# Moving the scan convolutions of six image pairs from TensorE to GpSimd

## The reference

```python
x = x + softmax(q @ k.T / 8) @ v                 # L0: attention over channels
x = relu(bn(deformable_conv3x3(x)))              # L1: offsets and mask from a 3x3 convolution
x = x + proj(softmax(q.T @ k / 8) @ v)           # L2: attention over the 256 pixels
# L3
y = depthwise3x3(layernorm2d(x)) + dw_b
for each of 4 directions (left-right, right-left, top-bottom, bottom-top):
    o += (conv1d_depthwise_5taps(y) + b) * sigmoid(y @ gate_w + gate_b)   # the "scan"
x = x + fuse(o)
x = x + ff2(a * sigmoid(g)),  a, g = split(ff1(layernorm2d(x)))
```

## Time and profile before

| | |
|---|---|
| time, median of 3 runs | 303.65 us (303.19 to 303.67) |
| span of the profiled execution | 301.8 us; the median lies 1.85 us above it |
| PE busy | 287.8 us (95%) |
| DVE busy | 213.0 us (71%) |
| ACT busy | 190.4 us (63%) |
| POOL busy | 53.0 us (18%) |
| TensorE clock granted | full in all 40 slices |
| from issue to landing, a load and a store of 128 KB (median) | 2.1 and 1.7 us |
| chain that ended last | PE 85%, DVE 5%, ACT 5%, POOL 1% |

### The profile page before, as it was taken

The page is one execution under the profiler, slowest core; times in us unless marked ns, Lnnn a source line. Parts: engine busy times, 40 slices in busy tenths (PEclk is TensorE's granted clock), DMA queues, the critical chain, the costliest instruction groups (busy, mean ns, idle before and its releaser), DMA issues.

```text
span 301.8 us, 7399 instructions
## 1 busy us (share of the span) xinstructions
PE 287.8 (95%) x2870; PEld 183.7 (61%) x2870; DVE 213.0 (71%) x424; ACT 190.4 (63%) x399; POOL 53.0 (18%) x139
## 2 busy tenths in 40 slices
...
DMA packets 3057, 4.98 MB, mean 16 GB/s; under 512 B 336, under 2 KB 2768, under 8 KB 2896
## 3 DMA queue, kind: packets, MB, share of 16 engines
...
...
HBM read 3.47 MB, written 1.05 MB: 15 GB/s over the span
## 4 chain that ended last, share of the span: by engine, by line
PE 85%; DVE 5%; ACT 5%; issue 3%; POOL 1%; ACTq 0%; POOLq 0%; DVEq 0%
PE ps_cv L534 22%; PE ps_pair L615 11%; PE ps_yb L494 8%; PE ps_pair L480 7%; PE ps_ma L437 6%; PE ps_ma L464 4%; PE ps_mb L580 3%; PE ps_pair L602 3%; PE ps_pair L570 3%; PE ps_mb L591 3%; PE ps_mb L547 3%; PE ps_mb L388 2%; PE ps_pair L635 2%; PE ps_mb L624 2%; PE ps_yb L374 1%
## 5 line engine op out<-in xcount | busy, mean ns | idle before, releaser
L901 DVE TENSOR_TENSOR sb_wt<-ps_yb,sb_xe 128x512 f32<-128x512 f32 x144 | 94.0, 684 | 26.4 <-PE ps_xb L489 24.9
L534 PE MATMUL ps_cv<-sb_wt,sb_w_x 128*64 128x256 f32 x576 | 77.3, 385 | 0.0
L740 ACT ACTIVATE sb_xe<-ps_xb 128x512 f32<-128x512 f32 x72 | 43.0, 597 | 19.3 <-PE ps_xb L489 19.2
L534 PEld LDWEIGHTS ps_cv<-sb_wt,sb_w_x 128*64 128x64 f32 x576 | 38.2, 136 | 20.2 <-issue 7.5
L615 PE MATMUL ps_pair<-sb_y_pad,sb_par 64*128 64x256 f32 x320 | 37.4, 383 | 0.3 <-ACT sb_gates L799 0.3
L615 PEld LDWEIGHTS ps_pair<-sb_y_pad,sb_par 64*128 64x128 f32 x320 | 30.9, 184 | 5.8 <-issue 2.5
L942 DVE SCALAR_TENSOR_TENSOR sb_dw_acc<-sb_z_pad,sb_par,sb_dw_acc 128x256 f32<-128x256 f32 x56 | 25.2, 480 | 9.4 <-ACT sb_dw_acc L792 5.3
L494 PE MATMUL ps_yb<-sb_hats,sb_sel 32*128 32x512 f16 x144 | 29.8, 383 | 0.7
L1039 POOL TENSOR_TENSOR sb_parts<-sb_hat,sb_parts 128x256 f16<-128x256 f32 (+2 forms) x40 | 23.3, 615 | 38.7 <-ACT sb_parts L710 38.6
L1046 POOL TENSOR_SCALAR sb_sc<-sb_mv 128x1 f32<-128x1 f32 x16 | 3.0, 190 | 142.1 <-DVE sb_mv L936 74.7
L489 PE MATMUL ps_xb<-sb_hats,sb_sel 32*128 32x512 f16 x72 | 27.7, 385 | 0.2 <-ACT sb_hats L719 0.2
(11 more groups left out here) (117 smaller groups left out, 438.4 us busy)
## 6 DMA issues: line engine op xcount, KB each, us to landing
...
```

The source lines that it names most:

```text
L534: mm = nc.tensor.matmul(cv[C * b:C * (b + 1), 0:PIX], w_x[n % 2][:, b, h, k, :], wt_of(n, k, h)[:, PIX * b:PIX * (b + 1)], start=(k == 0 a ...
L740: nc.scalar.activation(xe[t % XE][:, :], xb[:, :], ACT.Copy).then_inc(ev("xe_ok"), 1)
L901: nc.vector.tensor_tensor(wt_of(n, k, h)[:, :], yb[h][:, :], xe[t % XE][:, :], ALU.mult)\
```

## The change

For pairs 1 to 6 (`BY_POOL`) the scan is no longer done by PE and ACT. DVE writes `y` to a dense tile; SP issues four DMAs of 64 KB that put both images' channels on both halves of the partitions (`y_dup`); POOL then does for each of the two axes five multiply-and-add instructions by a column of weights (the first with the bias, straight into `conv`, the others into `tap_of` with a column of zeros added) and four additions into `conv`. That is 18 POOL instructions for a pair, each on 512, 480 or 448 elements for a partition. `prod` then waits for POOL's last addition on each axis. Pairs 7 and 8 keep their scans on PE.

Besides: `z_pad`, `dw_acc`, `y_pad`, `gates`, `conv`, `prod`, `z2`, `ff_a`, `ff_g`, `ff_u` get two buffers, `x4` three, `x2` eight, with the waits for freed buffers set accordingly; two more memsets on DVE at the start; `HOT` sums to 29 in place of 46, `WARM` to 22 in place of 21; and all lists of steps are written anew. In the new lists:

- DVE has `y.1` after `w5a.3` (before: after `w8a.3`), `y.6` after `w2a.8`, and behind the last weights `w8b.8`: `dw2.7 dw4.7 out.5 dw6.7 dw3.7 dw5.7 dw7.7 prod.6 max.8 x4.6 dw8.7`, later `dw7.8 dw8.8 y.8 prod.7`.
- POOL has each `ln1` inside the scan of the pair before, for instance `mul12.2 ln1.3 mul03.2 sum12.2 mul13.2 sum03.2 sum13.2 mul04.2 mul14.2 sum14.2 sum04.2`, and `low.5` to `low.8`, `ln2` and `x1` between or inside the scans.
- PE has `... sp_last.8 hot.1 ff2.5 s8a.8 s8b.8 gate.6 qk2.8 hot.2 logit.8 ...`: no `scan.6`, and `gate.6` behind the last sampling step.
- SP has `load.3 load.4 load.5 load.6 dup.1 dup.2 store.1 dup.3 load.7 dup.4 store.2 load.8 store.3 dup.5 dup.6 store.4 ...`.

```diff
+BY_POOL = (1, 2, 3, 4, 5, 6)
+ORDER = (2, 1, 3, 0, 4)
+SUMS = 2 * KS - 1
+            def dup(n):
+                sp.wait_ge(ev("y_ok"), n)
...
+                for b in range(2):
+                    for i in range(2):
+                        sp.dma_start(y_dup[n % 2][C * i:C * (i + 1), b, :, :].rearrange("p h w -> p (h w)"),
+                                     y[n % 2][C * b:C * (b + 1), :])\
+                            .then_inc(dup_ok[n % 2], 16)
...
+            def scan_times(d, i):
+                def step(n):
+                    rows, sum_of, tap_to = scan_rows(n, d, ORDER[i])
+                    weight = col("scan_c", KS * d + ORDER[i])
+                    if i == 0:
+                        pool.wait_ge(dup_ok[n % 2], 64 * len([k for k in BY_POOL if k <= n and (n - k) % 2 == 0]))
+                        wait_past(pool, ev("prod_ok"), n - 2)
+                        nc.gpsimd.tensor_scalar(sum_of, rows, weight, col("scan_b", d), ALU.mult, ALU.add)\
+                            .then_inc(ev(f"scan_step{d}"), 1)
+                    else:
+                        pool.wait_ge(ev(f"scan_step{d}"), scan_step(n, d, 2 * i - 2))
+                        nc.gpsimd.tensor_scalar(tap_to, rows, weight, col("none"), ALU.mult, ALU.add).then_inc(ev(f"scan_step{d}"), 1)
+                return step
+
+            def scan_plus(d, i):
+                def step(n):
+                    rows, sum_of, tap_to = scan_rows(n, d, ORDER[i])
+                    pool.wait_ge(ev(f"scan_step{d}"), scan_step(n, d, 2 * i - 1))
+                    nc.gpsimd.tensor_tensor(sum_of, sum_of, tap_to, ALU.add).then_inc(ev(f"scan_step{d}"), 1)
+                return step
...
             def prod_step(n):
+                wait_past(dve, ev("fuse_mm"), n - 2)
                 dve.wait_ge(ev("gate_ok"), n)
-                dve.wait_ge(ev("scan_ok"), n)
+                if n in BY_POOL:
+                    for d in range(2):
+                        dve.wait_ge(ev(f"scan_step{d}"), scan_step(n, d, SUMS - 1))
+                else:
+                    dve.wait_ge(ev("scan_ok"), made_by(BY_PE, n))
```

More of the change, by code:

```diff
@@ L60 @@
[L60 to L64, removed]
@@ L75 @@
[L75 to L78, removed]
+        warm.1 qk.1 warm.2 attn.1 warm.3 at.1 warm.4 mix.1 warm.5 x1.1 warm.6 off.1 prep.1 off_t.1 qk.2 wx0.1 attn.2
@@ L83 @@
[L83 to L96, removed]
+        attn.1 at.1 mix.1 off.1 prep.1 abs.1 tanh.1 attn.2 wx0.1 high.1 at.2 wx2.1 tr0.1 mix.2 xe0.1 tr1.1 xe1.1 tr2.1
@@ L97 @@
     """,
     "dve": """
[L99 to L102, removed]
@@ L113 @@
[L113 to L117 removed]
+        qk.1 a_max.1 a_norm.1 x1.1 dist.1 qk.2 a_max.2 hat.1 hat_y.1 a_norm.2 qk.3 low.1 x1.2 w0a.1 a_max.3 w0b.1 w1a.1
```

282 lines of the change are left out of this document (180 added, 102 removed).

## The result

The kernel with the change takes 310.3 us (median of 4 runs, 308.3 to 311.3), the kernel before 303.7 (4 runs, 303.2 to 304.5): a ratio of 1.021, 95% interval 1.018 to 1.023. It is slower, and the predicted 309 lies 1.3 us off. The profiled execution has a span of 308.0 us, against 301.8.

The account below looks back on a forecast made before the run. PE sets the pace before; afterwards DVE, waiting for POOL, was to bound the window. 301.8 + 8.7 - 4.7 + 2 = 307.8 us of span, plus 1.85 to the median about 309.7, said as 309; range 285 to 321.

Parts of the forecast that it names:

- window +8.7: From the first `y` to the last weights product: (124.7 + 29)/0.93 = 165.3 us, 8.7 us longer than before.
- tail -4.7 + 2: After the last weights product: 4.7 us less without a PE scan, plus 2 us for `prod.6` and `max.8` waiting.
- turns: POOL and DVE instructions reading two SBUF tensors, or scaling SBUF to SBUF, exclude each other, whole instruction by whole instruction.
- Rival 1: Two-input DVE instructions don't wait for POOL, only make it wait: 10 us of waits, time 288 us; chance 0.25.
- S: DVE's total added wait for POOL in the window: 29 us, with ends of 10 and 45 us.
- I let three in four meet: In the window, 26 of 35 `dw` taps meet a POOL instruction, each waiting 0.75 us: 19.5 us.
- rival 2: `dw` chains mostly miss POOL's scans: 18 us of DVE waits, window 153.4 us, time 298 us; chance 0.14.
- 93% of the window: DVE's busy share at its densest 30 us of before, taken as what it can fill of the whole window.
- the clock 0.03: Rival: PE's clock falls in its new gaps in window or tail, up to 15 us on the forecast; chance 0.03.
- the order, not the turns: Sign of a wrong prediction: DVE below 90% busy while PE too has gaps would point to the order of steps.
- Rival 3: POOL becomes the bound: 19.5 us a pair, `scan.6` ending near 275 us, time 315 to 320 us; chance 0.10.
- `prod.6`, `max.8`, +2: Behind the last weights product, `prod.6` waits some 2 us for POOL's `scan.6`, delaying `max.8` and pair 8's softmax: +2 us.

## Why the prediction was right, and where only its sum was

- **Where the time goes, as one sum.** Predicted: window +8.7, tail -4.7 + 2, span 307.8. Measured from 87.9 us on: +10.1 and -3.9, span 308.0. The sum holds, some of its terms don't, and two of them were wrong by 13 to 14 us each in opposite directions. That the span came out within 0.2 us is luck; that turns would eat the relief is not.
- **PE stops being the bound.** Right: 95% to 87% of the span, in the window 87%; I had written 80 to 85%.
- **GpSimd's price.** Right: multiplications 0.74 us in the median (0.77 said), additions 1.19 (1.04), a pair 17.8 us (16.7), busy 53%. The figure in the Trainium skill (GPSIMD Engine Reference, section 3, Performance versus the Vector engine), 4497 ns for 2048 elements, is 1.04 us for 474 in proportion; my estimate of 1.1 to 1.2 us from it needs a fixed part of 0.1 to 0.2 us beside. The trace agrees with the estimate, and with it the sum would have been a microsecond a pair nearer.
- **The turns.** The mechanism is right: taps and scalings wait for a whole instruction, the weights products don't; shorter instructions make shorter waits. Rival 1 falls. The size is off. S was 29 us, of which 19.5 from the taps: 26 of 35 at 0.75 us each. DVE's busy time rose by 16.5 us in the window, of which the taps have 9.4: 19 of 36 at 0.5 us each. So two terms of the sum were too large, "I let three in four meet" (half did) and the 0.75 us of a meeting. The 9.5 us for the other instructions were nearer (6 to 7). A mean of over 900 ns for the taps was wrong by that. By S alone this is rival 2, which gave 298.
- **What made up for it.** Two other steps failed the other way. I let DVE fill 93% of the window; it fills 85%. With 149.5 us of work the 93% would give 160.8 us, 14.4 less than measured. Most of this isn't the turns' doing: with GpSimd's instructions on one element the same sum falls short by 8.9 us (152.2 against 133.3/0.93), with memsets by 7.6 (160.9 against 142.6/0.93). The 93% came from 30 us of before, and no kernel here holds it through a window. And I gave the clock 0.03: it cost 6.7 us of matmul time, and filling the waits gave 3.3 us back and cuts the 14.4 to 11.0. What remains, some 2 us, fits waits on chains through POOL's queue (`low`, `ln2`) and DVE's held instructions; I can't divide it.
- **A sign of being wrong came up.** I had written that DVE below 90% while PE too has gaps would mean "the order, not the turns". After shows that: 85%, and 23.3 us of PE idle. The runs say both: the turns are there (16.2 us of DVE time that the one-element kernel doesn't have), and the waits of the engines for one another leave part of the window empty even without them.
- **GpSimd as the bound.** Rival 3 didn't come, but it is near: 5.7 us more a pair (17.8 to 23.5) made it true. I counted POOL by its busy time and left out that `ln` and `low` stand behind the scan in its queue.
- **`prod.6`, `max.8`, +2.** `prod` waits for ACT 0.3 us in all and never for POOL; the tail's -3.9 is between my -4.7 and -2.7.
